# The last layer's head loop: logit bursts one iteration ahead, first heads' steps moved up, and three output additions on GpSimd

## The chip, the cores and the metric

One core of a Trainium2 chip runs the whole program in one launch. The metric is device time in microseconds (us). PE is TensorE, DVE VectorE, ACT ScalarE, POOL GpSimd, and SP the engine whose queue issues nearly all the transfers of this part. A profiled execution gives the span from first to last instruction and the clock that TensorE was granted.

## What is computed

Four layers, each added to x (625 rows of 512) after a layernorm: a hyperbolic graph network, a mixture of experts, a plain graph network, and an attention block with a pooled memory. The change lies in the last of them (G = 8 groups, H = 16 heads in each, so 128 heads; L = 100 pooled rows; batch 1, s = 625):

```python
xn = _l2norm(x, d) * gamma_norm
q = (xn @ Wq_w + Wq_b).reshape(b, s, G, H, DQK)
kv = xn @ Wkv_w + Wkv_b
k, v = (kv[..., :G * DQK], kv[..., G * DQK:])
w = ...                                    # pooling weights from k, 625 x 100
kc = jnp.einsum('bsd,bsl->bld', k, w).reshape(b, L, G, DQK)
vc = jnp.einsum('bsd,bsl->bld', v, w).reshape(b, L, G, DV)
qk = jnp.einsum('bsghd,blgd->bghsl', q, kc) * (1.0 / DQK ** 0.5)
att = jax.nn.softmax(qk, axis=-1)
z = jnp.einsum('bghsl,blgd->bsghd', att, vc).reshape(b, s, G * H * DV)
zn = _l2norm(z, G * H * DV) * wz_g1
h1 = jax.nn.silu(zn @ wz_w1 + wz_b1)
h1n = _l2norm(h1, 2 * FF) * wz_g2
out = jax.nn.silu(h1n @ wz_w2 + wz_b2)
```

## The kernel before

The program is written for each engine by hand: `pe_ffn1`, `a_ffn1` (ACT), `v_ffn1` (DVE), `g_ffn1` (POOL) and `sp_ffn1` (SP) list their instructions in order, and named counters (semaphores) tie them. Nothing reorders them. Products want near float32 accuracy: an operand is split into a high part, rounded to the fast matmul type (by ACT), and a low part, the difference (by POOL or DVE), and three matmuls of the parts replace one.

The queries are never formed. For each head h, `m_(h)` multiplies the head's query weights by the pooled keys of its group (a 512 x 100 matrix, M): PE writes two PSUM banks (0 and 1), ACT copies half (MF), DVE `m_full` adds the rest, ACT `m_high` makes MH, POOL `m_low` makes ML. `burst(j)` then multiplies the 625 rows by the M of the four heads 4j to 4j+3: 60 matmuls of 400 columns in five row tiles, in PSUM banks 4 and 5; DVE adds a bias row from the tile CB (which came through DRAM: ACT's CR, a write to c_rows, a broadcast read) and takes the maximum of each head. After the burst a head goes through: `softmax_exp` (ACT, five exps), `softmax_end` (DVE, reciprocal and a 125 x 500 product on EE), `attT` (PE, five transposes into banks 2 and 3; ACT copies ATH, DVE takes ATL), `z_` (PE, six matmuls, again in banks 2 and 3; ACT takes ZH and the squares ZQ, DVE takes ZL, POOL adds the squares to ZS), and at last, for two heads together, `wz`: sixteen groups of six matmuls in banks 4 to 7 with the weights of `wz_w1` (WS), which DVE adds into ACC.

The head loop is a software pipeline over iterations i. An iteration does `z_(i-6)`, then `burst(i/4 - 1)` where i is a multiple of four from 4, `m_(i)`, eight `wz` groups (from i = 8), and between them `attT(i-5)`; ACT and DVE have `softmax_exp(i-4)` and `softmax_end(i-4)`. `piece(kind, b, k)` splits a quarter of a weight block of 1 MB: kind 0 is a block of query weights (four heads, tiles WQ, two sets), kind 1 a block of `wz_w1` (two heads, the gate pieces, tiles WS, from i = 6). The iterations 0 to 7 have no `wz`, and some other work in its place: the pooled keys (`keys(g)`: four before the loop, four in iterations 1 to 3), the pooled values (`values(c)`: 2 before the loop, 3 in iteration 4) and the bias rows (`bias_rows(b)`: 0 in iteration 0, 1 in iteration 4). These eight iterations are called the front below.

SP loads the blocks in the order in which sorted keys put them, four buffers in turn; a load waits until the block four before it has been split. After the loop comes the second matmul (`last`), whose five row tiles end in `stt` on DVE (scale, bias, into OT), Silu on ACT, an addition into X on DVE, and two stores each on SP.

## Time and profile before

| | |
|---|---|
| median of 3 runs | 2210.9 us (2210.38 to 2211.02) |
| profiled execution, its own time | 2215.61 us |
| span of its instructions | 2213.6 us |
| mean granted TensorE clock | 0.969 |
| busy: PE, PE weight loads, DVE, ACT, POOL | 2117.3, 1975.7, 1509.2, 1126.6, 854.7 us |
| front of the head loop, in the trace | about 601 to 677 us |

The granted clock is a share of the full clock: 1.00 is 2.4 GHz and 0.50 is 1.2 GHz. A row of the timeline that merges several instructions gives the start of the first and the time until the end of the last; matmuls overlap, so the next row starts before that end. In brackets stands how long the engine was idle before, and what ended it.

### The profile page before, as it was taken

What the parts mean: (1) busy time and instruction counts of PE and PEld (TensorE: products, weight loads), DVE (VectorE), ACT (ScalarE), POOL (GpSimd) and SP (SyncE); (2) the same over time, 40 slices, a digit from 0 to 9 for tenths busy, and PEclk for the clock granted to TensorE, in tenths of its full rate; (3) what the DMA queues carried; (4) which work ended last, traced back from release to release, by engine and by line L of the source; (5) the groups of instructions that cost most, each with busy time, mean ns of one, the idle gap of its engine ahead of it and who ended that gap; (6) DMA issues with size and microseconds to landing.
All of it is one profiled execution on the core that took longest, in us unless ns stands there. A gap on an engine that the chain in (4) does not pass through costs nothing.

```text
span 2213.6 us, 36119 instructions
## 1 busy us (share of the span) xinstructions
PE 2117.3 (96%) x13358; PEld 1975.7 (89%) x13358; DVE 1509.2 (68%) x3183; ACT 1126.6 (51%) x3010; POOL 854.7 (39%) x688
## 2 busy tenths in 40 slices
PE   8876799999879999999999999999999999999998
PEld 7765566668769999999999999999999999999997
DVE  8736688855436667777667767667777767777766
ACT  4534466542444455555455555455555545555554
POOL 0000000000045455555445555545555545555551
PEclk9886899999979999999999999999999999999999
DMA  6000588871022111122111121211122211112110
GB/s 209 1 19 4 175 279 288 272 270 51 10 79 80 62 62 62 66 99 73 69 61 62 61 97 67 81 62 62 61 73 92 81 62 62 62 62 100 62 44 24
DMA packets 85687, 197.42 MB, mean 89 GB/s; under 512 B 5937, under 2 KB 10321, under 8 KB 85511
## 3 DMA queue, kind: packets, MB, share of 16 engines
q1 hardware_dynamic: 85512, 195.12, 25.4%
q8 instruction: 106, 1.74, 0.3%
q14 instruction: 69, 0.57, 0.1%
HBM read 193.75 MB, written 1.35 MB: 88 GB/s over the span
## 4 chain that ended last, share of the span: by engine, by line
PE 89%; ACT 5%; DVE 4%; issue 1%; POOL 0%; DMA 0%; SPq 0%; DVEq 0%; POOLq 0%; ACTq 0%
PE PS L54 80%; PE PS L53 5%; PE PS L57 4%; ACT HW L88 1%; ACT GT L88 1%; ACT HS L88 0%; DMA X<-in_x 0%; DVE OHs L68 0%; POOL SM L60 0%; ACT EE L88 0%; DVE SM L107 0%; DVE OHd L69 0%; DVE M L75 0%; DVE JU L66 0%; DVE X L60 0%
## 5 line engine op out<-in xcount | busy, mean ns | idle before, releaser
L54 PE MATMUL PS<-ZH,WS 128*128 128x314 f32 x4096 | 946.8, 312 | 0.0
L54 PEld LDWEIGHTS PS<-ZH,WS 128*128 128x128 f32 x4096 | 691.9, 189 | 0.0
L54 PE MATMUL PS<-ZL,WS 128*128 128x314 f32 x2048 | 625.7, 305 | 0.0
L60 DVE TENSOR_TENSOR ACC<-ACC,PS 128x314 f32<-128x314 f32 x1008 | 476.8, 477 | 197.0 <-PE PS L54 187.1
L54 PEld LDWEIGHTS PS<-ZL,WS 128*128 128x128 f32 x2048 | 387.7, 189 | 0.0
L60 POOL TENSOR_TENSOR WS<-RAW,WS 128x512 fp32r<-128x512 f32 x256 | 327.0, 1298 | 109.7 <-ACT WS L88 109.6
L60 POOL TENSOR_TENSOR ML<-MF,MH 128x400 fp32r<-128x400 f32 x128 | 134.0, 1047 | 412.3 <-ACT MH L88 412.1
L60 POOL TENSOR_TENSOR ZS<-ZS,ZQ 128x628 f32<-128x628 f32 x128 | 198.3, 1549 | 235.3 <-ACT ZQ L88 235.3
L88 ACT ACTIVATE ZH<-PS,g1T 128x628 fp32r<-128x628 f32 x128 | 100.4, 785 | 321.7 <-PE PS L54 321.7
L88 ACT ACTIVATE EE<-EE,SM 125x100 f32<-125x100 f32 x640 | 233.3, 375 | 13.8 <-DVE SM L68 11.0
L88 ACT ACTIVATE MF<-PS 128x400 f32<-128x400 f32 x128 | 64.6, 505 | 319.7 <-PE PS L53 319.7
L75 DVE SCALAR_TENSOR_TENSOR ZL<-PS,g1T,ZH 128x628 fp32r<-128x628 f32 x128 | 111.7, 872 | 121.6 <-ACT ZQ L88 121.6
L60 DVE TENSOR_TENSOR EE<-PS,CB 125x400 f32<-125x400 f32 x160 | 92.0, 575 | 132.4 <-PE PS L54 131.8
L60 POOL TENSOR_TENSOR WQ<-RAW,WQ 128x512 fp32r<-128x512 f32 x128 | 167.2, 1306 | 0.4 <-ACT WQ L88 0.4
L60 DVE TENSOR_TENSOR EE<-EE,SM 125x500 f32<-125x500 f32 x128 | 155.3, 1214 | 4.4
L60 POOL TENSOR_TENSOR SM<-SM,hm 125x1 f32<-125x1 f32 (+1 forms) x9 | 7.8, 868 | 368.0 <-DVE SM L68 324.6
L88 ACT ACTIVATE WS<-RAW 128x512 fp32r<-128x512 f32 x256 | 147.5, 633 | 0.0
L54 PE MATMUL PS<-MH,XH 128*125 128x400 f32 x640 | 144.8, 348 | 1.6 <-POOL ML L60 1.6
L54 PE MATMUL PS<-MH,XL 128*125 128x400 f32 x640 | 143.8, 346 | 0.0
L54 PE MATMUL PS<-ML,XH 128*125 128x400 f32 x640 | 143.6, 346 | 0.0
L88 ACT ACTIVATE ATH<-PS 100x500 fp32r<-100x500 f32 (+1 forms) x256 | 96.3, 428 | 75.7 <-PE PS L57 75.7
L53 PEld LDWEIGHTS PS<-KCL,WQ 128*128 128x128 f32 x1024 | 131.4, 194 | 3.3 <-issue 3.0
(332 smaller groups left out, 3733.2 us busy)
## 6 DMA issues: line engine op xcount, KB each, us to landing
RAW<-in_L_ffn_wz_w SPq DMA_DIRECT2D x66, 1024.0 KB, 5.9
RAW<-in_L_ffn_w SPq DMA_DIRECT2D x64, 1024.0 KB, 7.3
RAW<-in_L_ffn_Wq_w SPq DMA_DIRECT2D x32, 1024.0 KB, 5.3
CB<-c_rows SPq DMA_DIRECT2D x32, 195.3 KB
RAW<-in_L_gnn_W SPq DMA_DIRECT2D x4, 1024.0 KB, 8.6
RAW<-in_L_ffn_Wkv_w SPq DMA_DIRECT2D x4, 1024.0 KB, 5.2
RAW<-in_L_ffn_Wk_T SPq DMA_DIRECT2D x2, 1024.0 KB, 6.0
WB<-w_rows SPq DMA_DIRECT2D x6, 305.2 KB
```

The source lines that it names most:

```text
L53: return self.q.matmul(o, l, r, start=start, stop=stop, skip_group_check=True)
L54: return self.q.matmul(o, l, r, start=start, stop=stop)
L57: return Nothing() if self.q is None else self.q.transpose(o, i, idn)
L60: return Nothing() if self.q is None else self.q.tensor_tensor(out=o, in0=a, in1=b, op=op)
L75: return self.q.scalar_tensor_tensor(out=o, in0=a, scalar=s, in1=b, op0=op0, op1=op1)
L88: return self.q.activation(o, i, f, **kw)
```

## The change

- In the loop on every engine `burst(j)` goes from iteration 4j+4 to 4j+3, and `m_`, with its ACT, DVE and POOL steps and the query pieces, one iteration up (`m_(i+1)` in iteration i). The loop begins at i = 3; what the iterations 0 to 2 did stands ahead of it.
- Heads 0 to 3 do `softmax`, `attT` and `z_` one iteration earlier than the formula of the others (`head_of`). In iterations 5 to 7 `attT` stands right behind `z_` (`early`), and the transposes of heads 1 to 3 go to banks 6 and 7 in place of 2 and 3.
- M of heads 1 and 3 goes to banks 4 and 5. The query pieces of heads 2 and 3 get tiles of their own and are split with those of heads 0 and 1, ahead of the pooling. ML of heads 0 to 3 is made on DVE (`first_low`) in place of POOL.
- `bias_rows(0)` goes ahead of `m_(0)`, `values(2)` behind `burst(0)` and `m_(4)`, `bias_rows(1)` to iteration 6.
- ACT and POOL split the first four gate pieces, those of block 0 (r = 0), ahead of their steps for M in iterations 6 and 7; before, they were behind them.
- SP: both first CB reads follow the first c_rows write at once; the query block of heads 4b to 4b+3 is loaded ahead of the `wz_w1` block that it came behind.
- At the end each row tile has an OT of its own; POOL adds tiles 0 to 2 into X, and DVE tiles 3 and 4 behind its last `stt`.

The core of the diff:

```diff
-        for _, kind, b in sorted([(4 * b - 1, 0, b) for b in range(32)] + [(2 * r + 6, 1, r) for r in range(64)]):
+        for _, kind, b in sorted([(4 * b - 2, 0, b) for b in range(32)] + [(2 * r + 6, 1, r) for r in range(64)]):
...
+        WQ += [[at(f"WQ{k}{p}", [128, 512], f32r, VO + 2048 * (2 * (k - 2) + p)) for p in range(2)] for k in (2, 3)]
...
+        OT1 = at("OT1", [P, T5, D], f32, VO)
...
+        def low_of(h):
+            return m_first.of(h) if h < 4 else m_lo.of(h)
...
+        FIRST, LAST = 3, NH + 7
+        def head_of(i, lag):
+            h = i - lag + 1
+            if not 0 <= h < 4:
+                h = i - lag
+                if not 4 <= h < NH:
+                    return None
+            return h
+        def at_bank(h):
+            return 6 if h in (1, 2, 3) else 2
+        def early(i):
+            return 4 < i < 8
         def burst_of(i):
-            return i // 4 - 1 if i % 4 == 0 and 4 <= i <= NH else None
+            return i // 4 if i % 4 == 3 and i < NH else None
+        def m_bank(h):
+            return 4 if h in (1, 3) else 0
...
-            q.wait_ge(*kv_mm.of("V", 2))
-            load(q, NFIRST + 2)
             q.wait_ge(*kc_hi.of("rows", 0))
+            q.wait_ge(*kc_lo.of(0))
             q.dma(crow[0:64, :].rearrange("(g h) l -> h g l", g=4), CR[:, :, :]).then_inc(s_cr, 16)
             q.wait_ge(s_cr, 16)
             rows_of(q, 0)
+            rows_of(q, 1)
+            q.wait_ge(*kv_mm.of("V", 2))
+            load(q, NFIRST + 2)
+            q.wait_ge(*kv_mm.of("V", 3))
+            load(q, NFIRST + 3)
             q.wait_ge(*ws_lo.of(0, 0, 3))
             load(q, NFIRST + 4)
-            q.wait_ge(*kv_mm.of("V", 3))
-            load(q, NFIRST + 3)
...
-            for i in range(LAST + 1):
-                if 0 <= i - 6 < NH:
-                    z_(i - 6)
-                if 2 <= i + 1 < NH:
-                    piece(0, (i + 1) // 4, (i + 1) % 4)
-                if i < NH:
-                    m_low(i)
-                if i == 4:
+            piece(0, 1, 0)
+            for i in range(FIRST, LAST + 1):
+                if i == 5:
                     q.wait_ge(*kv_mm.of("K", 7))
                     q.fill(ZS[:, :], 0.0).then_inc(*z_sum.up("zero"))
+                h = head_of(i, 6)
+                if h is not None:
+                    z_(h)
+                if i + 2 < NH:
+                    piece(0, (i + 2) // 4, (i + 2) % 4)
                 r, part = (i - 6) // 2, (i - 6) % 2
-                if 0 <= r < NH // 2:
+                if r == 0:
+                    piece(1, r, 2 * part)
+                    piece(1, r, 2 * part + 1)
+                if i + 1 < NH:
+                    m_low(i + 1)
+                if 1 <= r < NH // 2:
                     piece(1, r, 2 * part)
                     piece(1, r, 2 * part + 1)
...
+            for t in range(3):
+                q.wait_ge(*o_a.of(t))
+                q.tt(X[:, t, :], X[:, t, :], OT1[:, t, :], ALU.add).then_inc(*x4_g.up(t))
...
+            m_(0)
+            bias_rows(0)
+            for h in range(1, 4):
+                m_(h)
+                m_high(h - 1)
+            m_high(3)
+            piece(0, 1, 0)
+            keys(1)
+            for i in range(FIRST, LAST + 1):
+                h = head_of(i, 6)
+                if h is not None:
+                    z_(h)
+                if early(i):
+                    attT(head_of(i, 5))
+                if i + 2 < NH:
+                    piece(0, (i + 2) // 4, (i + 2) % 4)
+                r, part = (i - 6) // 2, (i - 6) % 2
+                if r == 0:
+                    piece(1, r, 2 * part)
+                    piece(1, r, 2 * part + 1)
+                h = head_of(i, 4)
+                if i == 4:
+                    softmax_exp(h)
+                if i + 1 < NH:
+                    m_(i + 1)
+                if h is not None and i != 4:
+                    softmax_exp(h)
+                if i + 1 < NH:
+                    m_high(i + 1)
+                if i == 3:
+                    values(2)
+                if i == 6:
+                    bias_rows(1)
+                if i == LAST:
+                    continue
+                h = head_of(i, 5)
+                if h is not None and not early(i):
+                    attT(h)
                 if i == 4:
                     values(3)
-                    bias_rows(1)
-                if 0 <= i - 4 < NH:
-                    softmax_exp(i - 4)
-                if i < NH:
-                    m_high(i)
-                if i == 0:
-                    bias_rows(0)
-                if i == 3:
-                    keys(1)
-                if i == LAST:
-                    continue
-                if 0 <= i - 5 < NH:
-                    attT(i - 5)
...
+            def first_low(h):
+                q.wait_ge(*m_hi.of(h))
+                q.tt(ML[:, :, h, :], MF[h % 2][:, :, :], MH[:, :, h, :].bitcast(f32), ALU.subtract).then_inc(*m_first.up(h))
+            for h in range(4):
+                m_full(h)
+                if h:
+                    first_low(h - 1)
+            first_low(3)
+            for i in range(FIRST, LAST + 1):
                 todo = wz_todo(i)
-                if 0 <= i - 6 < NH:
-                    z_(i - 6)
+                h = head_of(i, 6)
+                if h is not None:
+                    z_(h)
+                if early(i):
+                    att_lo(head_of(i, 5))
+                if i == 4:
+                    softmax_end(head_of(i, 4))
                 if burst_of(i) is not None:
                     burst(burst_of(i))
...
-            def add(t):
+            for t in range(T5):
+                q.wait_ge(*o_mm.of(t))
+                q.stt(OT1[:, t, :], PS[0:P, 2 + t, :], r5[:, t:t + 1], OB[:, :], ALU.mult, ALU.add).then_inc(*o_v.up("b", t))
+            for t in range(3, T5):
                 q.wait_ge(*o_a.of(t))
-                q.tt(X[:, t, :], X[:, t, :], OT1[:, t % 2, :], ALU.add).then_inc(*x4_done.up(t))
-
-            for t in range(T5):
-                q.wait_ge(*o_mm.of(t))
-                if t >= 2:
-                    q.wait_ge(*x4_done.of(t - 2))
-                q.stt(OT1[:, t % 2, :], PS[0:P, 2 + t, :], r5[:, t:t + 1], OB[:, :], ALU.mult, ALU.add).then_inc(*o_v.up("b", t))
-                if t:
-                    add(t - 1)
-            add(4)
+                q.tt(X[:, t, :], X[:, t, :], OT1[:, t, :], ALU.add).then_inc(*x4_done.up(t))
...
+            m_(0)
+            m_(1)
+            keys(4)
+            m_(2)
+            keys(5)
+            m_(3)
+            keys(6)
+            keys(7)
+            for i in range(FIRST, LAST + 1):
                 todo = wz_todo(i)
-                if 0 <= i - 6 < NH:
-                    z_(i - 6)
+                h = head_of(i, 6)
+                if h is not None:
+                    z_(h)
+                if early(i):
+                    attT(head_of(i, 5))
                 if burst_of(i) is not None:
                     burst(burst_of(i))
-                if i == 4:
-                    values(3)
+                if i + 1 < NH:
+                    m_(i + 1)
+                if i == 3:
+                    values(2)
+                if i == 6:
                     bias_rows(1)
-                if i < NH:
-                    m_(i)
-                if i == 0:
-                    bias_rows(0)
-                if 1 <= i < 4:
-                    for g in ((4, 5), (6,), (7,))[i - 1]:
-                        keys(g)
+                    free[4] = kc_hi.of("rows", 1)
```

ScalarE, the second softmax and the first transposes. Before (iteration 5 and the start of 6), from the query piece of head 6 to the squares of `z_(0)`:

```order
L88 ACTIVATE WQ_169<-RAW_63 128x512
L88 ACTIVATE MF_176<-PS 128x400 [waits m_hi,m_lo,m_mm]
L88 ACTIVATE EE_167,SM<-EE_167,SM 125x100 x5
L88 ACTIVATE MH<-MF_176 128x4x100 [waits m_v]
L88 ACTIVATE ATH<-PS 100x500 [waits pool_v,at_t]
L88 ACTIVATE ATH<-PS 100x125
L88 ACTIVATE ZH<-PS,g1T 128x628 [waits z_mm]
L88 ACTIVATE ZQ<-PS 128x628 [waits z_sum]
```

Now (iterations 4 and 5), from the same piece to the copies of head 1's transposes:

```order
L88 ACTIVATE WQ_168<-RAW_63 128x512
L88 ACTIVATE EE_166,SM<-EE_166,SM 125x100 x5
L88 ACTIVATE MF_175<-PS 128x400 [waits m_hi,m_first,m_mm]
L88 ACTIVATE MH<-MF_175 128x4x100 [waits m_v]
L88 ACTIVATE ATH<-PS 100x500 [waits pool_v,at_t]
L88 ACTIVATE ATH<-PS 100x125
L88 ACTIVATE VCH<-PS 100x512 [waits kv_mm]
L88 ACTIVATE ZH<-PS,g1T 128x628 [waits z_mm]
L88 ACTIVATE ZQ<-PS 128x628 [waits z_sum]
L88 ACTIVATE ATH<-PS 100x500 [waits at_t]
L88 ACTIVATE ATH<-PS 100x125
```

The exps of head 1 (x5) were behind MF of head 5 and now stand ahead of it; the copies of head 0's transposes (ATH) and the second VCH lie between MH of head 5 and ZH of head 0, and head 1's transposes are copied right behind ZQ of head 0.

TensorE, the first transposes (`ident,EE`). Before, `attT(0)`, `z_(0)` and the start of `m_(6)`:

```order
L57 MATMUL PS<-ident,EE_167 100x125 [waits sm_v]
L57 MATMUL PS<-ident,EE_167 100x125 x4
L54 MATMUL PS<-ATH,VCH 128x314 [waits at_lo]
L54 MATMUL PS<-ATL,VCH 128x314
L54 MATMUL PS<-ATH,VCL 128x314
L54 MATMUL PS<-ATH,VCH 128x314
L54 MATMUL PS<-ATL,VCH 128x314
L54 MATMUL PS<-ATH,VCL 128x314
L53 MATMUL PS<-KCL,WQ_169 128x200 [waits m_v,ws_lo]
L53 MATMUL PS<-KCL,WQ_170 128x100
```

Now, `attT(0)`, `values(3)`, `z_(0)`, `attT(1)` and the start of `m_(6)`:

```order
L57 MATMUL PS<-ident,EE_166 100x125 [waits kc_hi,sm_v]
L57 MATMUL PS<-ident,EE_166 100x125 x4
L54 MATMUL PS<-RAW_61,XP 100x512 [waits s_raw1]
L54 MATMUL PS<-RAW_61,XP 100x512 x3
L54 MATMUL PS<-KBR,CSr 100x512
L54 MATMUL PS<-ATH,VCH 128x314 [waits vc_lo,at_lo]
L54 MATMUL PS<-ATL,VCH 128x314
L54 MATMUL PS<-ATH,VCL 128x314
L54 MATMUL PS<-ATH,VCH 128x314
L54 MATMUL PS<-ATL,VCH 128x314
L54 MATMUL PS<-ATH,VCL 128x314
L57 MATMUL PS<-ident,EE_166 100x125 [waits vc_lo,sm_v]
L57 MATMUL PS<-ident,EE_166 100x125 x4
L53 MATMUL PS<-KCL,WQ_168 128x200 [waits m_v,ws_lo]
```

`values(3)` now lies between the transposes and the product that needs them, and the transposes of head 1 come ahead of `m_(6)`, with a wait for VCL in place of one for ZL.

VectorE, the end of the program (`OT` is the output tile). Before:

```order
L75 SCALAR_TENSOR_TENSOR OT_204<-PS,SM,OB 125x512 [waits o_mm,s_ob,o_v]
L75 SCALAR_TENSOR_TENSOR OT_204<-PS,SM,OB 125x512 [waits o_mm]
L60 TENSOR_TENSOR X<-X,OT_204 125x512 [waits o_a]
L75 SCALAR_TENSOR_TENSOR OT_204<-PS,SM,OB 125x512 [waits x4_done,o_mm]
L60 TENSOR_TENSOR X<-X,OT_204 125x512 [waits o_a]
L75 SCALAR_TENSOR_TENSOR OT_204<-PS,SM,OB 125x512 [waits x4_done,o_mm]
L60 TENSOR_TENSOR X<-X,OT_204 125x512 [waits o_a]
L75 SCALAR_TENSOR_TENSOR OT_204<-PS,SM,OB 125x512 [waits x4_done,o_mm]
L60 TENSOR_TENSOR X<-X,OT_204 125x512 [waits o_a] x2
```

Now, the same place, and then the last rows of GpSimd:

```order
L68 TENSOR_SCALAR SM<-SM 125x5 [waits o_v]
L75 SCALAR_TENSOR_TENSOR OT_209<-PS,SM,OB 125x512 [waits o_mm,s_ob,o_v]
L75 SCALAR_TENSOR_TENSOR OT_209<-PS,SM,OB 125x512 [waits o_mm] x4
L60 TENSOR_TENSOR X<-X,OT_209 125x512 [waits o_a] x2
```

```order
L60 TENSOR_TENSOR SM<-SM,hp 125x5 [waits rz_v]
L60 TENSOR_TENSOR SM<-SM,hp 125x5 [waits o_v]
L60 TENSOR_TENSOR X<-X,OT_209 125x512 [waits o_a] x3
```

Three of the additions into X have left VectorE, and its `stt` of one tile no longer waits for the addition of an earlier one.

## Rows read from the trace of the kernel before

**Rows 1.** The page: busy time of the engines, and two groups of instructions.

```profile
PE 2117.3 (96%) x13358; PEld 1975.7 (89%) x13358; DVE 1509.2 (68%) x3183; ACT 1126.6 (51%) x3010; POOL 854.7 (39%) x688
...
L88 ACT ACTIVATE EE<-EE,SM 125x100 f32<-125x100 f32 x640 | 233.3, 375 | 13.8 <-DVE SM L68 11.0
...
L60 POOL TENSOR_TENSOR WQ<-RAW,WQ 128x512 fp32r<-128x512 f32 x128 | 167.2, 1306 | 0.4 <-ACT WQ L88 0.4
```

**Rows 2.** Busy time by stage; the last, 748 to 796 us, is one steady loop period.

```profile
core 0: us, PE busy (x) PEld busy (x) DVE busy (x) ACT busy (x) POOL busy (x), PEclk, DMA share, GB/s
601.00:619.00 18.00, 15.87 (x95) 11.60 (x95) 4.20 (x9) 9.07 (x18) 8.33 (x8) 1.00 0.39 130
619.00:623.00 4.00, 4.00 (x16) 3.92 (x15) 1.15 (x2) 0.00 (x0) 0.84 (x1) 0.57 0.01 2
...
640.00:667.00 27.00, 16.57 (x62) 14.97 (x63) 11.86 (x20) 18.85 (x60) 19.86 (x16) 0.50 0.22 76
...
748.00:796.00 48.00, 48.00 (x331) 47.92 (x330) 33.66 (x67) 25.50 (x78) 25.75 (x21) 1.00 0.20 71
```

**Rows 3.** Who waited for whom, PE alone, 600 to 680 us.

```profile
PE PS L54 <- DVE ATL L60: 7.2, 3, 2.7
PE PS L57 <- DVE EE L60: 1.8, 1, 1.8
PE PS L53 <- DVE MF L60: 1.8, 2, 1.3
PE PS L57 <- DVE ZL L75: 1.8, 2, 0.9
PE PS L54 <- POOL ML L60: 1.6, 1, 1.6
```

**Rows 4.** Timeline of PE, head loop: start us, us, engine, line, op, names, count.

```profile
601.01 3.68 PE L54 MATMUL PS<-RAW,XP 128*100 128x512 f32 x8
...
661.25 0.63 PE L54 MATMUL PS<-ATH,VCH 100*128 100x314 f32 x1 [2.26 <-DVE ATL L60]
...
676.74 0.37 PE L54 MATMUL PS<-ZH,WS 128*128 128x314 f32 x1
...
759.89 0.31 PE L54 MATMUL PS<-ATH,VCH 100*128 100x314 f32 x1
...
760.76 0.89 PE L54 MATMUL PS<-MH,XH 128*125 128x400 f32 x4
...
771.72 0.99 PE L53 MATMUL PS<-KCL,WQ 128*128 128x200 f32 x8
```

**Rows 5.** Timeline of DVE in the front.

```profile
644.51 0.87 DVE L60 TENSOR_TENSOR ATL<-PS,ATH 100x500 fp32r<-100x500 f32 x2 [2.12 <-ACT ATH L88]
...
645.51 0.68 DVE L60 TENSOR_TENSOR EE<-EE,SM 125x500 f32<-125x500 f32 x1
...
648.82 0.87 DVE L75 SCALAR_TENSOR_TENSOR ZL<-PS,g1T,ZH 128x628 fp32r<-128x628 f32 x1 [2.62 <-ACT ZQ L88]
...
653.42 1.53 DVE L60 TENSOR_TENSOR EE<-EE,SM 125x500 f32<-125x500 f32 x1
```

**Rows 6.** Timeline of ACT in the front.

```profile
643.92 0.71 ACT L88 ACTIVATE ATH<-PS 100x500 fp32r<-100x500 f32 x2
...
648.10 0.69 ACT L88 ACTIVATE ZQ<-PS 128x628 f32<-128x628 f32 x1
```

**Rows 7.** Timeline of POOL in the front.

```profile
653.14 2.94 POOL L60 TENSOR_TENSOR WS<-RAW,WS 128x512 fp32r<-128x512 f32 x2
```

**Rows 8.** Transfers issued between 700 and 2100 us, median us to landing last.

```profile
RAW<-in_L_ffn_wz_w SPq DMA_DIRECT2D x59, 1024.0 KB, 6.9
```

**Rows 9.** Waits of ACT, 700 to 2100 us: total, times, longest.

```profile
ACT ZH L88 <- PE PS L54: 298.1, 117, 2.6
```

**Rows 10.** Timeline of all engines, the end of the program.

```profile
2207.84 0.39 PE L54 MATMUL PS<-W,H1L 128*125 128x512 f32 x1
...
2208.46 0.75 DVE L75 SCALAR_TENSOR_TENSOR OT<-PS,SM,OB 125x512 f32<-125x512 f32 x1
```

127 lines of the change are left out of this document (60 added, 67 removed).

## The prediction

> **What bounds the kernel now.** The page comes first: PE is busy for 96% of the span, its weight loads for less, the others for 68% and under [rows 1]. The stages come next, since an average hides them. In a steady loop period PE is busy for all of its 48 us at full clock [rows 2]. Nothing that is only reordered there can shorten it, and the change adds no matmul and removes none. So a gain must lie where PE waits or runs at half clock, and the front of the loop is that place. PE's waits between 600 and 680 us add up to 7.2 + 1.8 + 1.8 + 1.8 + 1.6 = 14.2 us [rows 3]. The granted clock was 0.57 from 619 to 623 and 0.50 from 640 to 667, during 4.0 and 16.57 us of busy PE [rows 2]; work at 1.2 GHz takes twice its time at 2.4 GHz, so 4.0 x 0.43 + 16.57 / 2 = 10.0 us were lost to it. From 601.01, the start of `values(2)`, to the first `wz` at 676.74 [rows 4] pass 75.7 us, of which 24.2 are waits or clock. The rest, 51.5 us, is matmul time at full speed and stays.
>
> Each fall of the clock came after waits: the first after PE had stood for 1.6 us for ML [rows 3], the second after waits for MF, EE and ATL; it stayed low while three iterations stood for ATL (7.2 us in all [rows 3]), and rose at 667, some 6 us after the last of these waits had ended at 661.25 [rows 2, 4].
>
> **The change, part by part.** I follow PE through the new order, with durations at full clock: a `z_` takes 760.76 - 759.89 = 0.87 us, a burst 771.72 - 760.76 = 10.96, an `m_` about 0.85 (its 0.99 less the overlap with what follows) [rows 4]; `values` 4.6, from 3.68 for its eight passes and about 1.0 for the bias [rows 4]. Five transposes take 0.6, an estimate between 0.45 (start to start inside steady work) and 1.28 at half clock.
>
> *Head of the front.* `bias_rows(0)` now waits for ACT's copy of the keys and `m_(0)` for DVE's low part, as `values(2)` no longer covers them. The nearest row is PE's wait for MF, 1.3 us at most [rows 3]; I take 1.05 for both together, between 0.5 and 1.8. The wait of 1.6 for ML goes: the query pieces of heads 0 to 3 lie ready, two PSUM pairs let `m_(1)` and `m_(3)` follow at once, and DVE, otherwise idle, makes ML. By my chain ML of head 3 is there at 611.9 and PE, with four `keys` still to do, reaches `burst(0)` at 612.3. The four pieces more during the layernorm lie in gaps of ACT and POOL: nothing. `burst(0)` runs to 623.25, `m_(4)` and `values(2)` to 628.7, `m_(5)` and `attT(0)` to 630.2, `values(3)` to 634.8. DVE's last sums, five exps (5 x 0.375 [rows 1]), reciprocal and product of head 0 end at 628, under `values(2)`: the waits for MF and EE (1.8 and 1.8) go.
>
> *First transposes.* ACT copies ATH of head 0 only behind the exps of head 1, `m_(5)` and MH, at 633.9; ATH takes 0.71 and ATL 0.87 from the end of its first part [rows 5, 6], so ATL ends at 635.4 and `z_(0)` waits 0.55. It ends at 636.3. `attT(1)`, in banks of its own, no longer waits for ZL (that 1.8 goes; 0.1 is left for VCL). For `z_(1)` ACT must make ZH and ZQ of head 0 (0.8, 0.69), DVE then ZL (0.87) and ATL of head 1 (0.87) [rows 5, 6]: 3.3 us, against 1.6 of PE work (`attT(1)`, `m_(6)`). **`z_(1)` waits 1.7**, to 639.6. `attT(2)` needs head 2's exps, which ACT starts at 639.35 behind ATH, a piece and MF: exps, reciprocal and product end at 642.25, **a wait of 1.75**. `attT(3)` needs the same of head 3, on ACT behind ZH, ZQ, ATH, a query piece, two gate pieces (put ahead of M by this change) and MF: exps from 645.7 to 647.6, and the product at 1.53, not 0.68 us, since POOL works beside it, as in the front now [rows 5, 7]. It is ready at 649.4, a wait of up to 3.7. ML of head 7 on POOL, behind two gate pieces (2.94 [rows 7]), is ready at 649.6, so `burst(1)` has it. At full clock the waits are 1.05 + 0.55 + 0.1 + 1.7 + 1.75 + 0.35 (`z_(2)`) + 3.7 = 9.2 us.
>
> *Clock.* From 637.9 to 642.25 PE stands for 3.45 us, more than before the first fall, so I let the clock fall at about 641 and rise at 655, 5 us after work becomes unbroken. Then `attT(2)` takes 0.6 more, `m_(7)`, `bias_rows(1)` and `z_(2)` stretch into waits that were there anyway, `attT(3)` takes 0.6 more and ends at 650.65, and 4.3 us of `burst(1)` at half clock cost 2.2. `burst(1)` ends at 663.8, then `m_(8)`, `z_(3)` and `m_(9)` (2.55): first `wz` at 666.4. The sum says the same: 51.5, 2.3 for the `z_`, `attT` and `m_` that come earlier, 6.15 of waits and 5.9 of clock make 666.9. I take 666.6. Before, the same work would have been done at 676.74 + 2.3 = 679.0: **12.4 us gained**.
>
> *Loop.* Per iteration every engine has the same instructions. A burst an iteration ahead gives the exps of its first head 9 us more, but PE never waited there: zero. SP reads the bias rows well ahead. The gate block of each even pair is now loaded behind the query block: cost zero, with a rival below.
>
> *End.* The last `stt` started 2208.46 - 2208.23 = 0.23 us after PE's last matmul; without additions between, I put it 0.1 us earlier. It is followed by Silu and two additions as before [rows 10]. POOL's three additions, at 1.3 us as its query pieces of like size take (1.47 in the front beside DVE [rows 1, 7]), run from about 2204.85 to 2208.75 or 2209.25, and DVE's first starts at 2209.1, behind the last `stt` of 0.75 us: gain 0.1, from 0.1 to a loss of 0.9. Here a rule speaks against the change. The Trainium skill, SBUF — State Buffer on-chip working memory, section Who interferes with whom, says that a DVE operation with two SBUF inputs and a GpSimd operation that reads SBUF exclude each other for their whole length. The trace agrees in the front: 0.68 alone and 1.53 beside POOL [rows 5, 7]. By the rule the end would be later only if POOL is still adding at 2209.1.
>
> The sum is 12.5 us. The profiled execution took 2215.61 us (span 2213.6), 4.7 above the median of 2210.9; so 2203.1 for a profiled execution, and **2198.4 us** for the median.
>
> **The rivals.**
> 1. *The clock stays at 2.4 GHz.* For it: the waits are apart, with work between. Against: one of 1.6 us was enough at 617. Only the 9.2 us of waits remain: gain 24.2 - 9.2 + 0.1 = 15.1, 2195.8 us.
> 2. *The front's chain is longer.* The clock also falls soon after 602, when PE has just stood for 1.05 us: 1.7 us as in 619 to 623. And products of heads 1 and 2 take 1.53 in place of 0.68, as POOL's pieces and ML may meet them: 1.7. Together 2201.8 us. For it: DVE's order is tight; against: POOL is idle when I have those products.
> 3. *The lock at the end.* POOL's third addition runs into DVE's first: +0.9, 2199.3 us. By the page on SBUF named above this is the rule's outcome if Silu or the stores delay POOL by 0.3 us.
> 4. *The change doesn't reach the wait.* `burst(1)` and `attT(3)` stay behind ACT's longer queue, so that the waits only change names: with the 10 us of clock unchanged and 2 us of waits saved, about 2208 us, no change.
> 5. *Slower: late gate blocks.* The load of an even pair's block now goes out in iteration 4k+1, when the fourth query piece is split, and ACT reads it in 4k+2, some 10.5 us later. A load of this kind lands in 6.9 us [rows 8]. From 10.5 ACT stands, and from 2.6 more (its idle time before ZH [rows 9]) PE too, in 30 periods. A landing of 14 us would cost 0.9 x 30 = 27: 2225 us. It decides from about 13.5 on, twice what is seen.
>
> **How the numbers follow.** My forecast gets 0.56, rival 1 0.15, rival 2 0.19, rival 3 0.03, rival 4 0.03, rival 5 0.04. The range reaches from just under rival 1, 2195.0, to just over rival 2, 2202.4; with the forecast's own spread these hold about 8 in 10 after what each size may miss. A measurement of this kernel can tell 0.2% (4.4 us) from no change: faster is under 2206.5. Forecast and rivals 1 to 3 lie there, 0.93; same 0.03; slower 0.04.
>
> **What would show it.** Right: `burst(0)` starts about 6 us earlier and without a wait; no PE wait on EE of head 0 nor on ZL; waits of 1 to 4 us on ATL and EE for heads 1 to 3; one stretch at clock 0.50 of 12 to 16 us, not 27; first `wz` near 666.6; steady periods still full. Wrong: a wait of PE in steady periods, ACT idle before WS for a transfer, a second stretch at half clock, or POOL's additions still running when DVE's begin.

## The result, and the profile after

| | before | changed |
|---|---|---|
| median of the timed runs | 2210.96 us (6 runs, 2210.33 to 2215.71) | 2202.42 us (6 runs, 2198.18 to 2203.1) |
| ratio, with its 95% interval | 1 | 0.9951 [0.9939, 0.9963] |
| profiled execution, its own time | 2215.61 us | 2201.53 us |
| span, mean granted clock | 2213.6 us, 0.969 | 2199.6 us, 0.973 |

The change makes the kernel faster: the two medians lie 8.5 us apart, the ratio, which uses all the runs, gives 10.8 us of 2210.96 (8.2 to 13.5 by its interval), and from profile to profile it is 14.1 us. The forecast was 2198.4 with a range from 2195.0 to 2202.4. The direction held, and the median lies on the upper bound of the range, 4.0 above the forecast.

The stages first, as in [rows 2]. Busy time by stage of the changed kernel; the columns are those of [rows 2]:

```profile
core 0: us, PE busy (x) PEld busy (x) DVE busy (x) ACT busy (x) POOL busy (x), PEclk, DMA share, GB/s
612.00:640.00 28.00, 26.06 (x126) 19.31 (x124) 13.54 (x26) 13.50 (x47) 8.69 (x8) 0.99 0.27 98
640.00:653.00 13.00, 11.17 (x45) 9.79 (x44) 6.01 (x11) 10.92 (x31) 11.40 (x9) 0.50 0.26 57
653.00:680.00 27.00, 26.64 (x178) 26.38 (x178) 16.77 (x34) 11.53 (x36) 13.43 (x12) 1.00 0.27 95
740.00:788.00 48.00, 48.00 (x330) 47.91 (x330) 33.66 (x67) 25.40 (x78) 25.70 (x20) 1.00 0.21 71
```

The half-clock stretch at 619 to 623 is gone, and the long one is about 13 us in place of 27. The steady period is as full as it was. Then PE's waits from 600 to 680 us in the changed kernel, against the 14.2 of [rows 3]:

```profile
PE PS L54 <- DVE ATL L60: 1.9, 2, 1.6
PE PS L57 <- DVE EE L60: 1.8, 2, 1.0
PE PS L54 <- ACT KCF L88: 0.6, 1, 0.6
PE PS L53 <- DVE KCL L60: 0.4, 1, 0.4
PE PS L53 <- DVE MF L60: 0.4, 1, 0.4
```

They add up to 5.1. ML and ZL no longer appear, and EE is another wait than before: it is that for heads 2 and 3, not for head 0. The timeline of PE in the changed kernel says where each stands (compare [rows 4]; the first row is the bias of the last `keys` ahead of the loop):

```profile
599.89 0.46 PE L54 MATMUL PS<-CSr,KBR 1*128 1x100 f32 x2
600.95 0.86 PE L54 MATMUL PS<-KCF,bqT 128*16 128x100 f32 x8 [0.59 <-ACT KCF L88]
602.22 1.96 PE L53 MATMUL PS<-KCL,WQ 128*128 128x200 f32 x16 [0.41 <-DVE KCL L60]
...
611.58 1.00 PE L54 MATMUL PS<-MH,XH 128*125 128x400 f32 x4
...
634.49 0.41 PE L54 MATMUL PS<-ATH,VCH 100*128 100x314 f32 x1 [0.33 <-DVE ATL L60]
...
638.79 0.41 PE L54 MATMUL PS<-ATH,VCH 100*128 100x314 f32 x1 [1.58 <-DVE ATL L60]
...
641.37 1.28 PE L57 MATMUL PS<-ident,EE 125*100 125x125 f32 x5 [1.00 <-DVE EE L60]
...
648.38 1.28 PE L57 MATMUL PS<-ident,EE 125*100 125x125 f32 x5 [0.83 <-DVE EE L60]
649.32 1.68 PE L54 MATMUL PS<-MH,XH 128*125 128x400 f32 x4
...
664.25 1.07 PE L53 MATMUL PS<-KCL,WQ 128*128 128x200 f32 x8 [0.36 <-DVE MF L60]
665.15 0.37 PE L54 MATMUL PS<-ZH,WS 128*128 128x314 f32 x1
```

`burst(0)` starts at 611.58 without a wait, `z_(0)`, `z_(1)`, `attT(2)` and `attT(3)` wait as the prediction says and in its order, `burst(1)` starts at 649.32 without a wait, and the first `wz` is at 665.15.

**Where the time went.** PE's instructions are the same in both kernels up to the last `keys` ahead of the loop (the row of two matmuls `CSr,KBR` at 599.89; the same row before starts at 600.62), and from there to its last one it does the same matmuls in another order. I use these two points for every kernel below. Before, PE's last matmul starts 2207.84 - 600.62 = 1607.2 us after the mark [rows 10]; now it starts 2193.90 - 599.89 = 1594.0 after it: **13.2 us gained in between**. The same comes out of the rows. Waits and clock were 24.2; now the waits are 5.1, and the clock, counted as the prediction counts it, takes 11.17 / 2 + 26.06 x 0.01 = 5.9; 24.2 - 5.1 - 5.9 = 13.2. To the 14.1 of the two profiles 0.7 is added ahead of the mark, and about 0.1 at the end.

The end of the program, all engines, in the changed kernel:

```profile
2190.85 3.80 POOL L60 TENSOR_TENSOR X<-X,OT 125x512 f32<-125x512 f32 x3 [2.16 <-ACT OT L88]
...
2193.90 0.39 PE L54 MATMUL PS<-W,H1L 128*125 128x512 f32 x1
2194.33 0.75 DVE L75 SCALAR_TENSOR_TENSOR OT<-PS,SM,OB 125x512 f32<-125x512 f32 x1 [0.65 <-PE PS L54]
2195.00 1.47 DVE L60 TENSOR_TENSOR X<-X,OT 125x512 f32<-125x512 f32 x2
```

POOL's additions end at 2194.65, 0.35 before DVE's begin. The last `stt` starts 0.04 after PE's last matmul has ended, not 0.23.

Last, the transfers. First the issues from 700 to 2100 us in the changed kernel (median us to landing last), then ACT's largest wait in the same stretch (total, times, longest), to be compared with [rows 8] and [rows 9]:

```profile
RAW<-in_L_ffn_wz_w SPq DMA_DIRECT2D x61, 1024.0 KB, 6.9
RAW<-in_L_ffn_Wq_w SPq DMA_DIRECT2D x27, 1024.0 KB, 8.5
```

```profile
ACT ZH L88 <- PE PS L54: 297.9, 117, 2.6
```

The query blocks land later than the gate blocks, and later than before (8.5 us against 5.3). The likely reason is that both now go out close together; no run tests it. Nobody waits for either: PE is busy for all of the steady period, and ACT's idle time ahead of ZH is what it was.

### The profile page after: what moved, and what is told of

Its sections match the earlier page's. It is cut to its first block, busy times and chain, and to the rows that moved or that the text cites. A ratio compares the mean times of both kernels' runs of the same rounds, so it can differ in the third digit from the quotient of the medians.

```text
span 2199.6 us, 36145 instructions
## 1 busy us (share of the span) xinstructions
PE 2114.6 (96%) x13358; PEld 1972.6 (90%) x13358; DVE 1507.6 (69%) x3184; ACT 1123.9 (51%) x3010; POOL 855.4 (39%) x687
## 4 chain that ended last, share of the span: by engine, by line
PE 90%; ACT 5%; DVE 3%; issue 1%; DMA 0%; POOL 0%; SPq 0%; DVEq 0%; POOLq 0%; ACTq 0%
PE PS L54 81%; PE PS L53 5%; PE PS L57 4%; ACT HW L88 1%; ACT GT L88 1%; ACT HS L88 1%; DMA X<-in_x 0%; POOL SM L60 0%; DVE OHs L68 0%; DVE SM L107 0%; ACT EE L88 0%; DVE OHd L69 0%; DVE M L75 0%; DVE JU L66 0%; DVE ACC L60 0%
```

## The experiments

Each kernel is made from the changed one, or from the one before where it says so. The table has the median of its runs, the ratio to the kernel before run beside it, and from its profile the time from the mark to PE's last matmul and the length of the stretches in the front in which the granted clock was 0.50.

| kernel | median (runs), ratio [95%] | mark to last matmul | half clock in the front |
|---|---|---|---|
| before | see above | 1607.2 | 3.4 + 27.3 |
| changed | 2202.42 (6), 0.9951 [0.9939, 0.9963] | 1594.0 | 13.6 |
| tail_only | 2211.34 (10), 0.9996 [0.9987, 1.0006] | 1608.2 | 6.8 + 27.3 |
| no_tail | 2201.23 (4), 0.9947 [0.9932, 0.9962] | 1592.3 | 6.8 |
| fill_after | 2200.19 (4), 0.9938 [0.9922, 0.9955] | 1592.0 | 0 |
| fill_before | 2208.68 (10), 0.9981 [0.9972, 0.9990] | 1601.7 | 3.4 |
| gates_behind | 2204.88 (7), 0.9962 [0.9950, 0.9975] | 1596.7 | 10.2 + 3.4 |
| banks23 | 2207.82 (10), 0.9974 [0.9965, 0.9984] | 1600.1 | 20.5 |
| heads_late | 2207.69 (10), 0.9974 [0.9965, 0.9984] | 1602.1 | 17.1 + 6.8 |
| low_pool | 2199.68 (4), 0.9942 [0.9927, 0.9957] | 1594.1 | 6.8 + 3.4 |
| exps_first | 2205.19 (4), 0.9957 [0.9943, 0.9971] | 1595.3 | 6.8 + 3.4 |
| exps_gates6 | 2197.04 (5), 0.9925 [0.9912, 0.9937] | 1591.6 | 6.8 |
| exps_gates6_fill | 2196.18 (5), 0.9917 [0.9903, 0.9930] | 1591.6 | 0 |

The kernel before, run beside them, had medians of 2213.16, 2213.25 and 2215.19 us in the three groups of runs (first four, next four, last three; the last group ran on another chip), so ratios are compared and not times. The third column comes from one profile each, and kernels with the same front differ in it by chance: before and tail_only lie 1.0 apart, changed and no_tail 1.7. A difference of 2 us or less in it is read together with the waits that caused it, or not at all.

### The end of the program: tail_only and no_tail

tail_only is the kernel before with the new end alone; no_tail is the changed kernel with all five additions on DVE again (each tile keeps an OT of its own):

```diff
-                q.wait_ge(*(x4_g if t < 3 else x4_done).of(t))
+                q.wait_ge(*x4_done.of(t))
...
-            for t in range(3):
-                q.wait_ge(*o_a.of(t))
-                q.tt(X[:, t, :], X[:, t, :], OT1[:, t, :], ALU.add).then_inc(*x4_g.up(t))
...
+            def add(t):
+                q.wait_ge(*o_a.of(t))
+                q.tt(X[:, t, :], X[:, t, :], OT1[:, t, :], ALU.add).then_inc(*x4_done.up(t))
+
             for t in range(T5):
                 q.wait_ge(*o_mm.of(t))
                 q.stt(OT1[:, t, :], PS[0:P, 2 + t, :], r5[:, t:t + 1], OB[:, :], ALU.mult, ALU.add).then_inc(*o_v.up("b", t))
-            for t in range(3, T5):
-                q.wait_ge(*o_a.of(t))
-                q.tt(X[:, t, :], X[:, t, :], OT1[:, t, :], ALU.add).then_inc(*x4_done.up(t))
+                if t:
+                    add(t - 1)
+            add(4)
```

> The kernel before with the end of the change alone (five output tiles, POOL adds tiles 0 to 2). Theory: a gain of 0.1 us, from 0.1 less the last stt's delay, which no timing can tell from nothing; the last stt starts within 0.1 us of PE's last matmul in place of 0.23. Rival (the lock between DVE and POOL): POOL's third addition runs into DVE's first, which then takes about 1.5 us in place of 0.7, and the end comes 0.9 us later. The front must look as in the kernel before: first wz some 75.7 us after the start of values(2), clock at 0.50 for some 27 us. Its timed runs also show whether the kernel before has two levels of time (2210.4 to 2211.0 and about 2215) by chance of the execution; if they lie in the front, the length from values(2) to the first wz differs by some 4 us between profiles at the two levels.

> The changed kernel, with the output additions all on DVE between the stt as before. Theory: the whole gain of the change is in the front, so this takes the changed kernel's time plus 0.1 us, 2202.5, ratio 0.995 to 0.996. Rival: the output tiles are a good part of the gain (over 1 us): then over 2203.5 us at the same level of the other stages.

Measured: a ratio of 0.9996 with an interval that holds 1, and from PE's last matmul to the end of the span 5.6 us (tail_only), 5.8 (no_tail), 5.7 (changed) and 5.8 (before). The new end is worth 0.2 us at most, in either kernel. In tail_only too the last `stt` starts 0.04 us after PE's last matmul has ended, and POOL's additions end 0.35 before DVE's begin. So the gain is in the front. tail_only's own front, 1.0 us longer than that of the kernel before in an execution 2.3 us shorter, also answers the question of its expectation: the two levels of time don't come from the front. Where these two profiles part is shown in the last section.

### The clock: fill_after and fill_before

Both add idle matmuls of 400 columns (their result is read by nobody, and goes to PSUM banks that are free there) where PE would stand: 8 ahead of and 9 behind `z_(1)`, 18 behind `z_(2)` in fill_after, whose edit is shown; in fill_before 58 in all in iterations 4 to 8.

```diff
+            def fill(bank, n):
+                q.wait_ge(*free[bank])
+                for _ in range(n):
+                    q.mm(PS[0:P, bank, 0:400], XH[:, 0, 0:P], XH[:, 1, 0:400], True, True)
+
...
+                if i == 6:
+                    fill(5, 8)
                 if h is not None:
                     z_(h)
+                if i == 6:
+                    fill(5, 9)
+                if i == 7:
+                    fill(5, 18)
```

> The changed kernel with idle matmuls (400 columns, results never read, bank 5) in PE's waits of the front: 8 ahead of z of head 1, 9 ahead of the transposes of head 2, 18 ahead of those of head 3. Theory: the stretch at clock 0.50 from 638 to 653 comes from the waits and costs some 3 us net (the matmul time lost there, 5.9 us, less what then turns into waits); with the waits filled the clock stays at 1.00 and the first wz comes 2.5 to 3.5 us sooner after the last keys. Rival 1: the clock does not follow these waits, it falls all the same, and the idle matmuls cost up to 1 us. Rival 2: the clock stays up, but all of it turns into waits on ACT's exps: no gain.

> The kernel before with idle matmuls (400 columns, results never read) in PE's waits of the front: 8 ahead of burst 0, 6 ahead of and 8 behind m of head 5, 12 ahead of z of each of heads 0 to 2. Theory: of the 24.2 us of waits and clock in the front, 10.0 are the clock's; with the clock kept at 1.00 burst 0 and the start of burst 1 give back 3.7 us, and three z and three transposes some 1.3 us an iteration: 6 to 8 us less in all, 2203 to 2205 us, about as much as the whole change. Rival: the chain over ACT and DVE sets these iterations, the clock is only a sign of it, and filling gives back 3.7 us or less.

Measured: in fill_after the clock stays at 1.00 through the whole front. Its stage that answers to the half-clock stretch:

```profile
640.00:653.00 13.00, 12.77 (x82) 11.92 (x81) 7.08 (x13) 11.32 (x33) 11.98 (x10) 1.00 0.30 70
```

It gains 2.0 us on the changed kernel (1594.0 to 1592.0), where 13.6 us had run at half clock. PE's timeline in fill_after says why it is not more:

```profile
649.37 1.00 PE L54 MATMUL PS<-MH,XH 128*125 128x400 f32 x4 [0.16 <-POOL ML L60]
```

The last `keys` of this execution start at 600.31, so `burst(1)` starts 49.1 us after them; in the changed kernel 49.4. A PE at full clock comes to `burst(1)` only 0.4 earlier, as it now waits for ML of head 7. Of the 2.0, 1.6 arise between the start of `burst(1)` and the first `wz` (15.8 us in the changed kernel, 14.2 in fill_after), where the changed kernel still runs 3.6 us at half clock. no_tail says the same without any idle matmul: its half clock of 6.8 us ends before the burst, it takes 14.2 from there to the first `wz`, and its 1592.3 is 0.3 above fill_after. So half clock that ends before the burst costs next to nothing here. The timed ratios of these three (0.9951, 0.9947, 0.9938) can't be told apart. In fill_before the third stage of [rows 2] runs at 0.94 and not at 0.50, and the waits of PE from 600 to 680 us that are left are these:

```profile
PE PS L57 <- DVE ZL L75: 3.3, 2, 1.6
PE PS L54 <- DVE ATL L60: 1.7, 2, 1.1
PE PS L53 <- DVE MF L60: 0.5, 1, 0.5
PE PS L57 <- DVE EE L60: 0.3, 1, 0.3
```

It gains 5.5 us in the profile and 4.2 by the ratio (2.2 to 6.2 by its interval). That is below the 6 to 8 that the theory wanted; the profile lies above the 3.7 of its rival, while the ratio alone doesn't tell the two apart. The clock accounts for about half of the 10.0 us that the prediction lays to it, and the rest comes back as time in which PE stands for ZL and ATL. The changed kernel, at 13.2, gains well over what a nearly full clock alone gives the kernel before; and between the two filled kernels, where the clock hardly plays a part, the reordering is worth 1601.7 - 1592.0 = 9.7 us. It does the larger part.

### Parts of the front: heads_late, banks23, gates_behind, low_pool

heads_late keeps the bursts, M and `values` where the change puts them, but gives heads 0 to 3 their old iterations and banks:

```diff
         def head_of(i, lag):
-            h = i - lag + 1
-            if not 0 <= h < 4:
-                h = i - lag
-                if not 4 <= h < NH:
-                    return None
-            return h
+            h = i - lag
+            return h if 0 <= h < NH else None
 
         def at_bank(h):
-            return 6 if h in (1, 2, 3) else 2
+            return 2
 
         def early(i):
-            return 4 < i < 8
+            return False
```

(In ACT and DVE the exception for i == 4 goes too.) 

> The changed kernel with heads 0 to 3 one iteration later again (as all other heads, transposes in banks 2 and 3 at their old place), bursts still an iteration ahead. Theory: burst 0 starts as in the changed kernel, with no wait; but the three waits on ATL of some 2.3 us each come back, and the half clock with them (over 20 us of it): 5 to 8 us slower than the changed kernel, 2207 to 2210 us. Rival: the bursts ahead are most of the gain: within 3 us of the changed kernel.

Its waits of PE from 600 to 680 us:

```profile
PE PS L54 <- DVE ATL L60: 10.4, 3, 3.6
```

1607.2 - 1602.1 = 5.1 us of the 13.2 come from the bursts and M ahead alone; the waits on ATL are even longer than before (10.4 against 7.2 [rows 3]), one chain of transposes, copies and product for each of three heads. The early heads bring the other 8.1.

banks23 leaves all as changed, but puts the transposes of heads 1 to 3 into the banks of `z_`:

```diff
         def at_bank(h):
-            return 6 if h in (1, 2, 3) else 2
+            return 2
```

> The changed kernel with all transposes in banks 2 and 3. Theory: the transposes of heads 1, 2 and 3 stand right behind z and must now wait until ACT and DVE have emptied its banks (ZH, ZQ, ZL: 2.4 us), and everything behind them is late: 1.5 to 2 us more for each of three heads, and a longer stretch of half clock: 4 to 8 us longer from the last keys to the first wz. Rival: the waits on the exps of heads 2 and 3 cover it: under 2 us.

```profile
PE PS L57 <- DVE ZL L75: 7.9, 3, 2.7
PE PS L54 <- DVE ATL L60: 0.7, 2, 0.4
```

These are its waits of PE for ZL and ATL in the front. So `attT` behind `z_` needs banks of its own: without them each of the three transposes waits until DVE has read the `z_` before it, and 6.1 us of the gain are lost (1594.0 to 1600.1; the ratios' intervals don't meet). The half clock is 20.5 us long.

gates_behind splits the first gate pieces behind M again, on ACT and POOL:

```diff
-                if r == 0:
-                    piece(1, r, 2 * part)
-                    piece(1, r, 2 * part + 1)
                 if i + 1 < NH:
                     m_low(i + 1)
-                if 1 <= r < NH // 2:
+                if 0 <= r < NH // 2:
                     piece(1, r, 2 * part)
```

> The changed kernel with the first four gate pieces behind M's steps on ACT and POOL, as before. From the last keys to the first wz the changed kernel took 65.3 us with 13.6 us of half clock (63.6 with 6.8). Theory: ML of head 7 comes 2.5 us earlier, so the wait ahead of burst 1 shrinks by some 0.8; but the pieces of iteration 7 now stand behind MF of head 8, which comes after burst 1, so the first wz waits for WS: two copies and two differences (1.1 + 2.6 us) after MH of head 8, some 2.7 us. Net 1.5 to 3 us longer. Rival: WS is there in time as in the kernel before, and the length shrinks by 0.8.

The first `wz` in its timeline of PE:

```profile
661.55 0.54 PE L54 MATMUL PS<-ZH,WS 128*128 128x314 f32 x1 [3.04 <-POOL WS L60]
```

`burst(1)` is not later (643.74 - 595.13 = 48.6 us after the mark, against 49.4), but the first `wz` now waits 3.0 for the last piece, which stands on POOL behind ML of head 8, and that waits for `m_(8)` behind the burst. The cost is 2.7 us, of which 1.2 lie ahead of the first `wz` (66.4 us after the mark against 65.3) and 1.5 behind it, where the clock falls once more, for 3.4 us. By the ratio alone, 0.9962 [0.9950, 0.9975], it can't be told from the changed kernel; the wait of 3.0 in the trace is what shows it.

low_pool makes ML of heads 0 to 3 on POOL (`m_low`, ahead of its first query piece), not on DVE:

```diff
         def low_of(h):
-            return m_first.of(h) if h < 4 else m_lo.of(h)
+            return m_lo.of(h)
...
+            for h in range(4):
+                m_low(h)
             piece(0, 1, 0)
...
                 m_full(h)
-                if h:
-                    first_low(h - 1)
-            first_low(3)
```

> The changed kernel with ML of heads 0 to 3 on POOL. Theory: ML of head 3 ends about 1.2 us after MH in place of 0.6; PE still has keys to do, so burst 0 waits 0 to 0.6 us: no difference in time that can be told. Rival: POOL's ML was what held burst 0 (1.6 us before): then 1 us or more comes back as a wait of PE on ML.

`burst(0)` then waits 0.4 for ML, and the time from the mark is 0.1 more than in the changed kernel: nothing that can be told from it. What took away the 1.6 us for ML [rows 3] was the order (query pieces of four heads ready, two pairs of banks), not the engine.

### A better front: exps_first, exps_gates6 and exps_gates6_fill

With the change two waits for EE are left and ML of head 7 ends only just in time. Rows of DVE and POOL in the changed kernel:

```profile
640.64 0.68 DVE L60 TENSOR_TENSOR EE<-EE,SM 125x500 f32<-125x500 f32 x1
...
647.44 0.89 DVE L60 TENSOR_TENSOR EE<-EE,SM 125x500 f32<-125x500 f32 x1
```

```profile
640.95 1.26 POOL L60 TENSOR_TENSOR ML<-MF,MH 128x400 fp32r<-128x400 f32 x1 [1.05 <-ACT MH L88]
...
645.27 2.53 POOL L60 TENSOR_TENSOR WS<-RAW,WS 128x512 fp32r<-128x512 f32 x2
647.76 1.46 POOL L60 TENSOR_TENSOR ML<-MF,MH 128x400 fp32r<-128x400 f32 x1
```

ML of head 7 ends at 649.22, `burst(1)` starts at 649.32. exps_first puts the exps of heads 2 and 3 on ACT ahead of the pieces and of M (and the product on DVE ahead of M's sum):

```diff
                     attT(head_of(i, 5))
+                if i in (5, 6):
+                    softmax_exp(head_of(i, 4))
...
-                if h is not None and i != 4:
+                if h is not None and i not in (4, 5, 6):
                     softmax_exp(h)
...
                     att_lo(head_of(i, 5))
-                if i == 4:
+                if i in (4, 5, 6):
                     softmax_end(head_of(i, 4))
```

> The changed kernel with the exps of heads 2 and 3, and the reciprocal and product behind them, at the head of iterations 5 and 6 on ACT and DVE (ahead of the query piece, the gate pieces and M). Theory: PE's waits on EE (1.0 and 0.8 us) go, but ML of head 7 on POOL, behind two gate pieces, already ended only 0.1 us before burst 1 began, so burst 1 is held by it instead: a wait on ML appears and the length from the last keys to the first wz shrinks by less than 0.5 us. Rival: ML was not at its limit, and 1.5 us or more are gained.

```profile
647.80 0.88 PE L57 MATMUL PS<-ident,EE 125*100 125x125 f32 x5
651.95 1.70 PE L54 MATMUL PS<-MH,XH 128*125 128x400 f32 x4 [3.26 <-POOL ML L60]
```

In its timeline of PE `attT(3)` no longer waits (`attT(2)` still waits 0.5 for EE), and `burst(1)` waits 3.3 for ML. It starts 50.9 us after the mark, in the changed kernel 49.4 and in no_tail, with the same front, also 49.4: 1.5 us later, where the theory allowed a small gain. In all the profile is 1.3 us worse than that of the changed kernel, and the ratios can't be told apart. ML of head 7 is the end of a chain on ACT and POOL, and on both queues work stood ahead of it: on ACT the exps, a query piece and two gate pieces, on POOL again the pieces.

exps_gates6 adds to this that the gate pieces of iteration 6 go behind M again (those of iteration 7 stay ahead):

```diff
-                if r == 0:
+                if i == 7:
                     piece(1, r, 2 * part)
                     piece(1, r, 2 * part + 1)
...
-                if 1 <= r < NH // 2:
+                if 0 <= r < NH // 2 and i != 7:
                     piece(1, r, 2 * part)
```

> As exps_first, and the two gate pieces of iteration 6 behind M's steps on ACT and POOL, those of iteration 7 still ahead. Theory: both holders of burst 1 are gone: it starts 1 to 1.6 us sooner after the last keys than in the changed kernel (49.4 us), WS is still there in time, and the last matmul comes 1 to 3 us sooner (1594.0 us after the last keys in the changed kernel's profile with 13.6 us of half clock). Rival: the copies of the transposes (ATL) hold z all the same, and nothing is gained.

Its waits of PE from 600 to 680 us (those for KCF and KCL, 0.6 and 0.4 as in the changed kernel, lie ahead of 600 here):

```profile
PE PS L54 <- DVE ATL L60: 1.9, 2, 1.6
PE PS L54 <- POOL ML L60: 1.0, 1, 1.0
PE PS L57 <- DVE EE L60: 0.5, 1, 0.5
PE PS L53 <- DVE MF L60: 0.4, 1, 0.4
```

And its ML of head 7 in the timeline of POOL:

```profile
644.52 1.03 POOL L60 TENSOR_TENSOR ML<-MF,MH 128x400 fp32r<-128x400 f32 x1
```

It is the better front: its ratio, 0.9925 [0.9912, 0.9937], lies below the interval of the changed kernel, if barely, and from the mark to the last matmul it takes 2.4 us less than the changed kernel's profile. Against no_tail, which has the changed kernel's front, the profile is only 0.7 better and the intervals overlap, so the size of the gain is open. With KCF and KCL the waits are 4.8 in place of 5.1; `burst(1)` starts 0.8 us earlier after the mark (645.61 - 596.96 = 48.6), and the half clock, 6.8 us long, ends before it, so that the burst runs at full speed. The theory had 1 to 3 us, and 1 to 1.6 for the burst. exps_gates6_fill adds 20 of the idle matmuls (8, 4 and 8, their result unread) to it.

> As exps_gates6 with 8, 4 and 8 idle matmuls (results never read) ahead of z of head 1 and of the transposes of heads 2 and 3. Theory: no half clock in the front at all, and 1.5 to 2 us less than exps_gates6 where that has 7 to 14 us of half clock: about 1591 us from the last keys to the last matmul. Rival: with fewer waits the clock stays up by itself, and the idle matmuls cost up to 1 us.

The clock stays at 1.00, and the time from the mark is the same (1591.6): the 1.5 to 2 us of its theory did not come, as `burst(1)` starts 48.7 us after the mark in both and waits 0.9 for ML even so. The timed ratio is 0.9917 [0.9903, 0.9930], not to be told from that of exps_gates6. Here the clock falls only where PE would wait anyway, and keeping it up buys nothing in the front.

## Why the prediction was right, point by point

- **What bounds the kernel.** Right. The steady period is 48.00 busy of 48 in both, and the gain stands between the mark and the first `wz`. There 76.1 us became 65.3, with 2.3 us more work done in it: 13.2 where the prediction has 12.4.
- **Head of the front.** 1.05 was taken for KCF and KCL, 0.59 + 0.41 = 1.0 measured. `burst(0)` was put 612.3 - 600.62 = 11.7 us after the mark; it starts 611.58 - 599.89 = 11.7 after it. The waits for ML, for MF at 1.3 and for head 0's EE are gone.
- **First transposes.** Waits forecast with the clock falling, and measured: `z_(0)` 0.55, 0.33; VCL 0.1, none; `z_(1)` 1.7, 1.58; `attT(2)` 1.75, 1.00; `z_(2)` none, none; `attT(3)` 1.0 (what is left of the prediction's 6.15), 0.83. A wait for MF of 0.36 ahead of `m_(9)` was not forecast. Sum 6.15 against 5.1. The mis-sized term is `attT(2)`. Its product was ready 41.4 us after the mark, near the forecast 41.6; but the clock fell already within `z_(1)`, which took 1.6 and not 0.87, and so the wait began later. For `attT(3)` the product beside POOL took 0.89, not 1.53.
- **ML of head 7.** Forecast ready at 649.6, 49.0 after the mark, with `burst(1)` at 50.0; measured 49.3 and 49.4. The two are closer together than forecast, so that ML, not the transposes, is what the next improvement runs into (exps_first, fill_after).
- **Clock.** One fall, from about 639 to 653 instead of 641 to 655, and 5.9 us lost by the prediction's way of counting, as forecast. That the length came out is in part luck: in no_tail, with the same front, it was 6.8 us. Nor does half clock make these matmuls take twice their time. In the kernel before a row of four matmuls of a burst follows the one before it after 1.33 us at half clock and after 0.73 at full, 1.8 times:

```profile
662.99 1.53 PE L54 MATMUL PS<-MH,XH 128*125 128x400 f32 x4
664.32 1.53 PE L54 MATMUL PS<-MH,XL 128*125 128x400 f32 x4
...
668.61 0.89 PE L54 MATMUL PS<-ML,XH 128*125 128x400 f32 x4
669.33 0.90 PE L54 MATMUL PS<-MH,XH 128*125 128x400 f32 x4
```

By this the prediction's 10.0 us were about 9.0 and the 5.9 about 5.3, and the sum of the rows above comes to 12.8 instead of 13.2; 0.4 us remain that no row places. More important, this figure is not what the clock is worth: fill_after wins back 2.0, near the 2.6 by which rival 1 lay below the forecast, because most of the slow matmuls run in time in which PE would wait. The prediction allowed for this in the changed kernel ("stretch into waits that were there anyway") but its opening sentence on the kernel before did not: there 10.0 us are called lost to the clock, and fill_before wins back 5.5. The Trainium skill, TensorE: Matmul & The Clock Gate, section HAM oscillation — how this bites in real kernels, works out what a slow stretch costs as half its length. By that page the 13.6 us of the changed kernel would cost 6.8, an estimate, and the measured 2.0 speaks against using it where PE waits within the stretch.
- **The parts.** The prediction has no sum by part. The runs give: bursts and M ahead 5.1, early heads 8.1, of which 6.1 hang on the banks of their own; the gate pieces ahead 2.7; ML on DVE 0.1, which is nothing. Each is a difference of two profiles, good to about 1 to 2 us. These overlap and are not to be added up.
- **Loop.** Zero, right. Rival 5 (a late gate block) is out: the landing is 6.9 us as before, against the 13.5 from which it decides, and ACT's idle time ahead of ZH is unchanged.
- **End.** 0.1 forecast, 0 to 0.2 measured by tail_only and no_tail. Rival 3 (the lock) didn't come: POOL ends 0.35 us before DVE begins. The rule of the Trainium skill that was weighed there (SBUF — State Buffer, section Who interferes with whom) was not tested at this place. The page calls the shared ports an exclusive lock; that one side holds it for a whole instruction it says of DVE's 2-port modes, so the prediction's "for their whole length" reads more into it for these additions than it states.
- **Rivals 2 and 4** are out: no fall of the clock follows the wait at 602, the products of heads 1 and 2 took 0.68 each, not 1.53, and the waits did not change names only.
- **The number.** In the profile the gain is 14.1 where 12.5 was forecast; the median is 4.0 above the forecast. The weak step is the carrying over: the whole gain, worked out in an execution 4.7 us above the median of before, was taken off that median. The medians lie 8.5 apart; by the ratio it is 10.8 (8.2 to 13.5), by that of no_tail, with the same front, 11.7. Rival 2's 2201.8 lies nearer to the 2202.42 than the forecast does, though nothing of what it says came about, and it is the margin for rival 2 that carries the range as far as 2202.4. So the mechanism was right on its own account, and that the median still falls on the range is luck. Why the medians are nearer than the profiles was not settled, since no timed execution has a trace. The profiles offer a candidate, in the last section: two lengths, 3 us apart, of a stretch 100 us into the program that the change doesn't touch. Both profiles compared here had the longer one, and the median of before, 4.7 below its profile, may well come from executions with the shorter.

## What to carry to other kernels

Where a full engine is fed by chains on other engines, look for the gain in the ramp ahead of the steady loop, and follow each engine's own queue through it by hand, one instruction after the other; here that gave every wait to within 0.8 us, and missed one of 0.36. A stretch at half clock costs only what PE would not have waited anyway: count it against the chain that sets the next start, not as half of its busy time. And when one wait is taken away, move what stands ahead of the next product in the same queues too: exps_first alone made `burst(1)` start 1.5 us later after the mark, and with two gate pieces moved as well it started 0.8 earlier than in the changed kernel.

## What the runs showed of the hardware

- The same code ran with different half-clock stretches. Changed kernel and no_tail have one front: 13.6 and 6.8 us of it at half clock, 1594.0 and 1592.3 from the mark. Ahead of the mark, in code that is the same in the changed kernel and the nine made from it, the last `keys` start between 595.13 (gates_behind) and 601.04 us (exps_first). The kernel before took 2209.7 to 2216.4 us in the 50 runs beside the experiments. Differences of a few us between two single profiles say little, unless they are taken from a mark.
- About 3 us of this spread arise at one place. 94 us into the program, far ahead of the changed part, stands a row of 50 small matmuls. The changed kernel and then low_pool:

```profile
94.33 8.46 PE L53 MATMUL PS<-ones,CT 125*125 125x1 f32 x50
```

```profile
94.22 5.51 PE L53 MATMUL PS<-ones,CT 125*125 125x1 f32 x50
```

From 96 to 100 us the granted clock was 0.56 in the first and 0.97 in the second. Of the 13 profiles, six have the row at 7.8 to 8.5 us (before, changed, no_tail, fill_after, fill_before, exps_first), and their last `keys` start at 599.9 to 601.0; seven have it at 5.5 to 6.0, and start at 595.1 to 597.5. So the same code, with the clock falling over this row or not, ends up some 3 us apart. That the spread of the timed runs (2210 to 2211 and about 2215 us for the kernel before) comes from it is possible and not shown, as they have no trace.
- Idle matmuls in place of waits keep the granted clock at 1.00 in the whole front (fill_after, exps_gates6_fill), and what they win is at most 2.0, and nothing.
- DVE and POOL lengthen each other's instructions. Head 3's product on DVE takes 0.89 and the ML on POOL beside it 1.46, where they take 0.68 and, in exps_gates6, 1.03 alone; in the kernel before the product took 1.53 beside two gate pieces [rows 5, 7]. This agrees with the page of the Trainium skill named above (SBUF — State Buffer, Who interferes with whom), which lets a DVE instruction with two SBUF inputs and a GpSimd instruction that reads SBUF exclude each other; the lengthening, 0.21 and 0.43 us, is less than a whole instruction. A reading that fits the rows, and that no run tests, is that one of POOL's was nearly over when the product was ready (the gate piece before ML ends at 647.8, the product starts at 647.44).
